# Slot attention with a switch FFN on one core: the first group's closing sums and routing placed ahead of the second group's last half, the candidate product ahead of the experts, and the end copied in halves and gated on DVE

## The reference

```
slots = layernorm(x)
k, v = rmsnorm(ctx) @ Wk.T, rmsnorm(ctx) @ Wv.T
three times:
    q = rmsnorm(slots) @ Wq.T
    attn = softmax over the 512 slots of (q . k * SCALE)
    attn = attn / (sum over the 32 context rows + eps)
    u = attn @ v
    r = sigmoid(u@Wir + h@Whr + b);  z = sigmoid(u@Wiz + h@Whz + b)
    n = tanh(u@Win + b + r * (h@Whn + b));  h = (1 - z) * n + z * h
x = x + slots
t = layernorm(x);  logits = t @ Wg        (8 experts)
gate = softmax(logits) at its argmax;  pos = tokens before this one with the same choice
keep the token if pos < 64                (capacity)
out = x + gate * ( gelu_tanh(t @ W1[e]) @ W2[e] )     for kept tokens
```

## Time and profile before

| | us |
|---|---|
| median of 3 runs | 138.66 (138.54 to 139.07) |
| profiled execution | 138.64 |
| its span | 136.9 |
| busy: PE / PE weight loads | 124.2 / 89.0 |
| busy: DVE / ACT / POOL | 93.6 / 79.4 / 33.6 |

### The profile page before, as it was taken

One profiled execution on the slowest core, in us unless ns is written; L12 is line 12 of the kernel. 1 busy time (PEld: TensorE's weight loads), 2 busy tenths in 40 slices (PEclk: granted clock), 3 DMA queues, 4 the chain that ended last, 5 costly groups with the idle time before them and its releaser, 6 DMA issues.

```text
span 136.9 us, 2770 instructions
## 1 busy us (share of the span) xinstructions
PE 124.2 (91%) x1038; PEld 89.0 (65%) x1039; DVE 93.6 (68%) x304; ACT 79.4 (58%) x154; POOL 33.6 (25%) x54
## 2 busy tenths in 40 slices
PE   6999988999899998998978997699999999999950
PEld 2573843664664754754834943599999799987830
DVE  2797656996996996996997899974782041134751
ACT  1568383945855865765636678863694265315350
POOL 7633805005005005005000060027000065550000
PEclk9999999999999999999999999999999999999998
DMA  3989991000000000000000000000101201113115
GB/s 98 277 226 333 366 382 51 0 0 7 0 0 0 0 5 0 0 2 0 5 0 0 0 0 0 0 5 0 41 5 38 77 24 30 34 31 87 34 42 153
DMA packets 9197, 8.05 MB, mean 59 GB/s; under 512 B 601, under 2 KB 7028, under 8 KB 9184
## 3 DMA queue, kind: packets, MB, share of 16 engines
q1 hardware_dynamic: 8492, 7.28, 16.6%
q0 software_dynamic: 256, 0.40, 1.2%
q10 hardware_dynamic: 436, 0.20, 0.6%
HBM read 6.43 MB, written 1.57 MB: 58 GB/s over the span
## 4 chain that ended last, share of the span: by engine, by line
PE 71%; DVE 14%; ACT 9%; issue 3%; POOL 1%; ACTq 0%; DVEq 0%
PE ps L1302 11%; PE ps L1288 11%; PE ps L1144 6%; PE ps L1117 6%; PE ps L1136 5%; PE ps L1110 5%; PE ps L980 3%; PE ps L1314 3%; PE ps L1218 3%; ACT r_b L422 3%; PE ps L1063 3%; PE ps L1181 2%; PE ps L1093 2%; ACT z_b L436 2%; PE ps L1074 2%
## 5 line engine op out<-in xcount | busy, mean ns | idle before, releaser
L1144 PE MATMUL ps<-attn,VW 32*128 32x256 f32 x144 | 12.9, 426 | 3.5 <-DVE ps L712 2.0
L1288 PE MATMUL ps<-h,W_t 128*128 128x128 f32 x128 | 15.9, 279 | 0.0
L1288 PEld LDWEIGHTS ps<-h,W_t 128*128 128x128 f32 x128 | 15.0, 192 | 0.5 <-issue 0.3
L429 ACT ACTIVATE ps<-ps,half_b 128x512 f32<-128x512 f32 x12 | 7.9, 660 | 12.7 <-PE ps L1117 12.7
L1136 PE MATMUL ps<-h,whhT 128*128 128x256 f32 x48 | 13.7, 405 | 0.0
L1117 PE MATMUL ps<-h,whhT 128*128 128x256 f32 x48 | 13.3, 398 | 0.0
L346 POOL DMA_INDIRECT y_tok<-y_rows,row_of x8 | 8.3, 1034 | 18.9 <-DMA y_rows<-y_sb 14.1
L1144 PEld LDWEIGHTS ps<-attn,VW 32*128 32x128 f32 x144 | 5.6, 182 | 10.6 <-DVE ps L712 4.4
L1110 PE MATMUL ps<-h,whhT 128*128 128x256 f32 x48 | 11.7, 384 | 0.0
L422 ACT ACTIVATE r_b<-ps,half_b 128x512 f32<-128x512 f32 x12 | 7.6, 684 | 7.1 <-PE ps L1144 7.1
L712 DVE SCALAR_TENSOR_TENSOR ps<-r_b,ps 128x512 f32<-128x512 f32 x12 | 7.8, 693 | 5.1 <-ACT r_b L422 5.1
(11 more groups left out here) (168 smaller groups left out, 255.2 us busy)
## 6 DMA issues: line engine op xcount, KB each, us to landing
W_t<-in_L_ffn_W_dram SPq DMA_DIRECT2D x1, 2048.0 KB, 9.6
x_tok<-in_x_dram SPq DMA_DIRECT2D x4, 256.0 KB, 3.9
out_dram<-h SPq DMA_DIRECT2D x4, 256.0 KB, 2.3
y_rows<-y_sb SPq DMA_DIRECT2D x4, 128.0 KB, 1.8
n_b<-in_L_xattn_gru_whh_dram SPq DMA_DIRECT2D x1, 192.0 KB, 4.1
n_b<-in_L_xattn_gru_wih_dram SPq DMA_DIRECT2D x1, 192.0 KB, 3.5
y_tok<-y_rows,row_of POOLq DMA_INDIRECT x8, 3.7
n_b<-in_ctx_dram ACTq DMA_DIRECT2D x1, 64.0 KB, 2.9
```

The lines of the kernel that those rows point to most:

```text
L1144: last = mm(to[:, hf, :], VW[g][p:p + M, gate * P:(gate + 1) * P], attn[g][p:p + M, :], start=False, stop=True, skip_group_check=True)
L1288: last = mm(hid_bank[e][:, j * BG * CAP:(j + 1) * BG * CAP], W1_t[:, ex_, j * P:(j + 1) * P], rhs, start=True, stop=True)
```

## The change

**At half 4** (t = 2, g = 0) PE no longer issues `slots_z(1, 1, 2)`, and DVE issues `final_x(0)` and `final_x(1)` each behind its `new_slots`, ahead of the denominators of the last half.

**The last half**: on PE `x2_back(0)`, `x2_back(1)` and the first group's logits stand first, then `attn_r`. The update gate's products go by a new function, `last_update`, into banks 4 and 5, one batch at a time with `positions(0)` between; batch 2's waits for the update tanh of batch 3. Fourteen filler products become three. `attn_n` stands behind `dispatch(1)`. On DVE the first group's routing stands ahead of `reset_hn`, `kept_slots` and `weigh_n`. ACT does both resets and `update(1)` ahead of `x2_norm(0)`, and `update(0)` and the two candidates behind `dispatched_out(1)`, the second candidate between `gelu(0)` and `gelu(1)`.

**The experts**: `x_T(2)` and `x_T(3)` stand behind `up(1)`, and `final_x(2)` and `(3)` read x from PSUM, without ACT's copy. `x2_back(2)`, `x2_back(3)` and the second group's logits stand behind `down(0)`.

**The end**: batches 2 and 3 are both copied on ACT, in halves of 256 columns; the transposes wait for halves and go to two banks for each batch; all eight gated additions are DVE's; batch 3 is sent in two DMAs.

```diff
     HS = [(hf, i) for hf in range(2) for i in range(BG)]
+    SLOT_HALF = [slice(0, NH), slice(NH, N)]
     SQ = 32
...
         row_bank = [bank[4], bank[5]]
-        disp_bank = [bank[2], bank[3], bank[0], bank[1]]
+        disp_bank = [bank[6], bank[7], bank[0], bank[1]]
         x_bank = [bank[6], bank[7]]
         norm_bank = [ps[:, 6, :], ps[:, 7, :], ps[:, 6, :], None]
-        late_x_bank = [bank[1], bank[0]]
+        late_x_bank = [bank[4], bank[5]]
+        last_ZV = [ps[:, 4:6, NH:N], ps[:, 4:6, 0:NH]]
         vw_bank = [bank[2], bank[3]]
-        hid_bank = [bank[2], bank[3]]
-        y_bank = [bank[6], bank[7]]
-        back_bank = [bank[0], bank[1], bank[2], bank[3]]
+        hid_bank = [bank[6], bank[7]]
+        y_bank = [bank[2], bank[3]]
+        back_bank = [[bank[2], bank[3]], [bank[0], bank[1]]]
...
             return BG * g + i
+
+        def update_bank(g, i, t):
+            return last_ZV[i] if (g, t) == (NG - 1, ITERS - 1) else ZV[i]
...
                              y_sb[:, k, :, :]).then_inc(y_put, 16)
-            for b in range(B):
-                sp.wait_ge(fin, (C, 2 * C, 3 * C, 3 * C + 1)[b])
+            for b in range(B - 1):
+                sp.wait_ge(fin, C * (b + 1))
                 sp.dma_start(out[b].rearrange("(c p) d -> p c d", p=P),
                              res[:, b, :].rearrange("p (c d) -> p c d", d=D)).then_inc(out_done, 16)
-            sp.wait_ge(out_done, 16 * B)
+            for k in range(2):
+                cs = slice(2 * k, 2 * k + 2)
+                sp.wait_ge(fin, C * (B - 1) + 2 * k + 2)
+                sp.dma_start(out[B - 1].rearrange("(c p) d -> p c d", p=P)[:, cs, :],
+                             res[:, B - 1, :].rearrange("p (c d) -> p c d", d=D)[:, cs, :]).then_inc(out_done, 16)
+            sp.wait_ge(out_done, 16 * (B + 1))
...
                 act.wait_ge(xTp, b + 1)
-                nc.scalar.activation(xT[:, b, :], (x_bank[b] if b < 2 else late_x_bank[b - 2])[:, :],
-                                     ACT.Copy).then_inc(xTc, 1)
+                nc.scalar.activation(xT[:, b, :], x_bank[b][:, :], ACT.Copy).then_inc(xTc, 1)
...
                     act.wait_ge(S[1]["scP"], 1)
-                nc.scalar.activation(halves(z_b[:, b, :]), ZV[i], ACT.Tanh, bias=half_b[:, 1:2],
+                nc.scalar.activation(halves(z_b[:, b, :]), update_bank(g, i, t), ACT.Tanh, bias=half_b[:, 1:2],
                                      scale=0.5).then_inc(s["tz"], 1)
...
             t, g = ITERS - 1, NG - 1
+            x2_out(0)
+            x2_out(1)
             reset(g, 0, t)
...
             update(g, 1, t)
-            update(g, 0, t)
-            candidate(g, 0, t)
-            candidate(g, 1, t)
-            x2_out(0)
-            x2_out(1)
-            x_out(2)
-            x_out(3)
             x2_norm(0)
...
             x_high(1)
+            dispatched_out(0)
             gate_exp(0)
             gelu_table()
-            dispatched_out(0)
             dispatched_out(1)
...
                 if s == 1:
-                    act.wait_ge(x2T, B)
+                    act.wait_ge(S[0]["h_ready"], BG * (ITERS + 1))
                 if s >= 2:
...
                 act.wait_ge(accD, b - BG + 1)
-                nc.scalar.activation(oT[:, b, :], acc_bank[b % BG][:, :], ACT.Copy).then_inc(oTs, 1)
-
-            x2_out(2)
+                for cs in SLOT_HALF:
+                    nc.scalar.activation(oT[:, b, cs], acc_bank[b % BG][:, cs], ACT.Copy).then_inc(oTs, 1)
+
+            update(g, 0, t)
+            candidate(g, 0, t)
             gelu(0)
-            x2_out(3)
+            candidate(g, 1, t)
             gelu(1)
             y_out(0)
+            x2_out(2)
+            x2_out(3)
             x2_norm(2)
...
             summed_out(2)
-            act.wait_ge(gt, 2)
-            act.wait_ge(backP, B - BG)
-            for c in range(C):
-                n = (B - 1) * C + c
-                nc.scalar.activation(oT[:, B - 1, c * P:(c + 1) * P], back_bank[B - 1][:, c * P:(c + 1) * P],
-                                     ACT.Copy, scale=gate[:, n:n + 1]).then_inc(go, 1)
+            summed_out(3)
...
                 g, i = b // BG, b % BG
-                dve.wait_ge(xTc, b + 1)
+                dve.wait_ge(xTc if b < BG else xTp, b + 1)
                 dve.wait_ge(S[g]["h_ready"], BG * ITERS + i + 1)
-                v.scalar_tensor_tensor(out=xT[:, b, :], in0=h[:, b, :], scalar=0.5, in1=xT[:, b, :],
+                v.scalar_tensor_tensor(out=xT[:, b, :], in0=h[:, b, :], scalar=0.5,
+                                       in1=xT[:, b, :] if b < BG else late_x_bank[b - BG][:, :],
                                        op0=ALU.mult, op1=ALU.add).then_inc(x2T, 1)
...
                 new_slots(g, 0, t)
+                if (g, t) == (0, ITERS - 1):
+                    final_x(0)
                 new_slots(g, 1, t)
+                if (g, t) == (0, ITERS - 1):
+                    final_x(1)
                 inv_denominators(og, ot)
...
             t, g = ITERS - 1, NG - 1
-            final_x(0)
-            final_x(1)
-            reset_hn(g, 0, t)
-            reset_hn(g, 1, t)
-            kept_slots(g, 1, t)
-            kept_slots(g, 0, t)
-            weigh_n(g, 0, t)
             x2_stats(0)
...
             x_low(1)
+            reset_hn(g, 0, t)
+            reset_hn(g, 1, t)
+            kept_slots(g, 1, t)
+            kept_slots(g, 0, t)
+            gates(0)
+            weigh_n(g, 0, t)
             weigh_n(g, 1, t)
             new_slots(g, 0, t)
+            new_slots(g, 1, t)
             final_x(2)
-            new_slots(g, 1, t)
             final_x(3)
-            gates(0)
...
             def gated_out(b):
-                dve.wait_ge(backP, b - BG + 1)
                 for c in range(C):
                     n = b * C + c
-                    v.scalar_tensor_tensor(out=res[:, b, c * D:(c + 1) * D], in0=back_bank[b][:, c * D:(c + 1) * D],
+                    dve.wait_ge(backP, 2 * ((n - BG * C) // 2) + 2)
+                    v.scalar_tensor_tensor(out=res[:, b, c * D:(c + 1) * D], in0=back_bank[b - BG][c // 2][:, c % 2 * D:(c % 2 + 1) * D],
                                            scalar=gate[:, n:n + 1], in1=x2_tok[:, n, :],
...
             gates(1)
-            dve.wait_ge(accD, BG)
-            v.tensor_copy(oT[:, B - 1, :], acc_bank[BG - 1][:, :]).then_inc(oTv, 1)
             dve.wait_ge(gt, 2)
-            gated_out(B - 2)
-            dve.wait_ge(go, C)
-            v.tensor_tensor(res[:, B - 1, :], oT[:, B - 1, :],
-                            x2_tok[:, (B - 1) * C:B * C, :].rearrange("p c d -> p (c d)"), ALU.add).then_inc(fin, 1)
+            gated_out(2)
+            gated_out(3)
...
                 if b == 2:
-                    pe.wait_ge(S[1]["n"], BG * ITERS)
+                    pe.wait_ge(S[1]["tz"], BG * ITERS)
                 to = x_bank[b] if b < 2 else late_x_bank[b - 2]
...
                     pe.wait_ge(S[1]["h_ready"], 1)
-                mm(sum_ps, fold[:, :], esum[g][:, 0:1], start=(g == 0 and t == 0), stop=True,
+                mm(sum_ps, fold[:, :], esum[g][:, 0:1], start=(g, t) in ((0, 0), (NG - 1, ITERS - 1)), stop=True,
                    skip_group_check=True).then_inc(s["fold"], 1)
...
                     last = mm(den_ps[rows, :], einv[g][rows, 0:1].broadcast_to([M, M]), ex[g][rows, :],
-                              start=False, stop=True, skip_group_check=True)
+                              start=(g, t) == (NG - 1, ITERS - 1), stop=True, skip_group_check=True)
                 last.then_inc(s["den"], 1)
...
+            def last_update(i):
+
+                g, t, b = NG - 1, ITERS - 1, batch(NG - 1, i)
+                if i == 1:
+                    pe.wait_ge(x2c, BG)
+                else:
+                    pe.wait_ge(S[g]["tz"], BG * t + 1)
+                for hf in range(2):
+                    mm(last_ZV[i][:, hf, :], whhT[:, P:2 * P], h[:, b, hf * NH:(hf + 1) * NH], start=True, stop=False,
+                       skip_group_check=True)
+                attn_gate(g, i, 1, last_ZV[i]).then_inc(S[g]["zp"], 1)
+
             def attn_n(g, t):
...
-                if b < 2:
-                    pe.wait_ge(S[1]["tz"], BG * ITERS)
                 pe.wait_ge(x2T, b + 1)
...
                 if g == 0:
-                    pe.wait_ge(S[1]["tz"], BG * ITERS)
+                    pe.wait_ge(S[1]["einv"], ITERS)
                 else:
...
-                if b < BG:
-                    pe.wait_ge(S[1]["n"], BG * ITERS)
-                else:
+                if b >= BG:
                     pe.wait_ge(x2c, B)
...
                 attn_n(g, t)
-                slots_z(og, 1, ot)
+                if (og, ot) != (NG - 1, ITERS - 1):
+                    slots_z(og, 1, ot)
                 slots_r(og, 0, ot)
...
             t, g = ITERS - 1, NG - 1
-            attn_r(g, t)
-            slots_z(g, 0, t)
-            attn_z(g, t)
-            attn_n(g, t)
             x2_back(0)
...
```

(35 more changed lines are left out.)

## The result

The changed kernel took 137.19 us in the median of 4 runs (135.46 to 139.74), the kernel before 138.60: a ratio of 0.986 (0.982 to 0.991). Two later comparisons gave 0.976 (0.972 to 0.980) and 0.986 (0.981 to 0.991). The ratios leave out the disturbed runs of either kernel; here these are part of the finding, because most of them are the changed kernel's own, by a fall of TensorE's clock.

| mean clock | runs | us |
|---|---|---|
| 0.991 to 1.000 | 6 | 135.29 to 135.77 |
| 0.986, 0.987 | 4 | 136.56 to 137.60 |
| 0.951 to 0.954 | 6 | 139.74 to 141.57 |
| 1.000 | 1 | 137.72 |

A forecast was written before the change was run, and what follows sets the result against it. The prediction took PE's work from up(0) on as the bound: up(0) 4.6 us earlier leaves 1.8, the end gives 1.0, so 138.64 - 1.8 - 1.0 = 135.8 us. Range 134.7 to 138.7.

The forecast's parts named there:

- The sum: Whole kernel: 138.64 less 1.8 at the expert stretch and 1.0 at the end gives 135.8; chance 0.58.
- the 4.6 us: First group's routing ahead of attention's last half: up(0) starts at 84.7 where it was 89.33, 4.6 earlier.
- the loss to waits: Expert stretch: second group's chain up to gelu(3) makes PE wait 0.2, 0.1 and 0.6, the last ahead of down(3).
- The 1.6 of moved work: Expert stretch: x_T (1.1) and x2_back(2) (0.55) move into it and take 1.6 of the 4.6 gained.
- the likeliest case: The sum of 135.8 holds, own range 134.8 to 136.8; chance 0.58.
- rival B: Second group's serial chain to gelu(3) slips further, three operations 0.4 late make 1.2: 137.0; chance 0.18.
- rival C: Gelu's table doesn't serve tanh, so four table loads of 1.28 are added: 138.6, no change; chance 0.12.
- The narrow gate products of one batch: Last half's update gate on PE, ahead of positions(0): four narrow products, taken as about 0.45.
- The last DMA: Kernel's end: half as large, 128 KB in 1.8 against 256 KB in 2.3; bounds 0 and 0.5, taken as 0.3.
- The end in all: Copies, transposes and gated additions save 0.68 and the last DMA 0.3, together 1.0.
- My own sign of an error: The forecast is wrong if, among other signs, PE's granted clock is under 1.00 between 74 and 100.
- rival D: Added table loads idle PE, the clock drops to 1.2 GHz for up(1) and down(0): 142.3; chance 0.12.

The follow-up runs named there:

- The experiments on the chain: Changed kernel with three of four second-group normalization operations per batch left out: 135.07 without a fall; separately, with batch 2's shift inside choose(1): mean 135.09 without a fall.
- the run of the end alone: Kernel before with only the new end (half copies on ACT, gated additions on DVE, batch 3 in two DMAs): 137.91 median of 12, ratio 0.994.
- two of the later kernels: Changed kernel without the three fillers ahead of dispatch(0), profiled at 140.50; changed kernel with batch 2's shift moved inside choose(1), its slowest run 141.46.
- five kernels with fillers put back: Changed kernel with fillers in the narrow stretch, where PE waits, there plus early shift, in both narrow stretches plus shift, and more of them: upper-clock runs 134.91 to 136.88.
- four kernels without: The changed kernel, and it without fillers ahead of dispatch(0), with a shortened second-group normalization, or with batch 2's shift earlier: best runs 135.29, 135.71, 135.07, 134.78.
- the early shift: Changed kernel with DVE's shift for batch 2 inside choose(1), behind the subtraction: 134.78 to 135.28 in four runs without a fall; others 137.14, 139.24, 141.46.
- the kernel with most fillers: Kernel with early shift and fillers in gaps and both narrow stretches, raised to six between logits(0) and logits(1), four between logits(2) and logits(3): 136.32 to 136.88.

## Why the prediction was right, and where not

*The sum.* Without a fall, the kernel takes 135.3 to 135.8; predicted 135.8. The steps, measured in the run at 135.77: up(0) at 84.49 (84.7), normalization at 95.85 (96.23), gelu(3)'s end at 102.43 (102.8), down(3)'s at 104.45 (104.7), DVE's last end at 131.42 (131.7, which is 133.49 less the 1.8). Of the 4.6 us only 1.8 would be left at down(3), said the sum; 2.1 were. ACT's work from the normalization to gelu(3)'s end took 6.58, where I took 6.56; it began 0.4 earlier than I had it, and PE waited 0.32 ahead of down(3) and not 0.6. The experiments on the chain confirm the loss to waits. The 1.6 of moved work was not tried by itself.

*The median is not the sum's.* 137.19 lies in the range I gave, but outside the likeliest case's own 134.8 to 136.8, near rival B's 137.0. But B's slip of the second group's chain didn't come, since that chain ran 0.4 earlier than forecast, and neither did rival C, for which the range reached to 138.7. That the range holds the median is luck. For "faster" I had given 0.74; the comparisons came out 1.4, 2.4 and 1.4% below the kernel before, where the sum said 2.0%, and these ratios don't count the long falls.

*Mis-sized terms.* The narrow gate products of one batch (x4 records, two products; I called them four) take 0.70, all that those of both batches take (x8), where I took 0.45; place(0) still had room. The last DMA gave 0.1 where I took 0.3; why isn't shown, though others are in flight beside it. The end in all is 0.8 by the profiles (1.0), and 0.9 by the run of the end alone.

*Tables.* Rival C is out: one load serves gelu and the tanh behind it in every profile. Nothing in the old trace could say so. What the Trainium skill has on it ("ScalarE: Activation LUTs", "Table sets: the hidden batching unit") lists tanh with other sets and is silent on this one; "What ACT_TABLE_LOAD costs" has a switch at 2.66, load and drain, and here the load takes 1.28 and the next operation starts 0.01 behind it. The prediction's "some 4 us longer" by that figure is low, since four times 2.66 less 1.40 is 5.0; nothing else rests on it.

*The clock.* This is the step that failed: the sum holds only while the clock does, and I had no term for its loss apart from rival C's idle. I wrote that no idle of the new order was over 0.7 and took that as cover, and I tied a fall to rival C's idle. The clock fell without it, in 10 of 17 runs, and in the profiled one PE had no gap in the 2 us before; the last one was of 0.23, ahead of x2_back(1). My own sign of an error, a clock under 1.00 between 74 and 100, is what came. A short fall costs 1.6 (137.1 against 135.5), the runs with a long one 4.2 to 6.0, and both profiles at 0.951 (140.50 and 141.46 us, of two of the later kernels) have a short fall behind the long one. The prediction's range doesn't hold these runs. That removed fillers "had held the clock" I offered as a remark inside rival D, whose price is worked out with C's idle. What differs is this: the change put eight transposes and the logits' eight narrow products (x16) ahead of the gates, thinned the work behind them, and took 11 fillers out. In the old order the same narrow products stood behind the gates and ahead of eight more transposes and the fillers, and no run of it had a fall. In 29 runs of five kernels with fillers put back there was no long fall, in 38 runs of four kernels without there were 14. Short falls stayed (8 of the 29). Which of the two, the place of the logits or the thinner work behind them, brings the fall isn't separated: all five have two fillers behind x2_back(0), and four of them have more behind the gates too. The small waits of 0.23 and 0.25 that stand ahead of the first and the second fall are a rival that no run tries by itself. Against it speak the old order, where PE waits 0.24 ahead of the same transposes and logits, and the kernel with most fillers, which kept the 0.25: neither had a fall. So that the clock's fall makes the difference between the runs is shown, and that fillers rid the kernel of the long ones; what brings a fall on stays open.

## What to carry to other kernels

When work is reordered, add to the sum of waits a look at what PE does in each stretch of a few microseconds: a row of PE that is busy all the time, with narrow products, is no proof that the clock will hold. Take the distribution, not one profile: the changed kernel's mean over 17 runs was 137.9, its profile without a fall 135.8. And compare kernels by all their runs: with the early shift, fillers made the best run 0.6 slower and the mean of six runs 0.9 faster than that of seven without. And when an early start is won, follow the next serial chain over the engines to the product that needs it, before counting the gain.

## What the runs showed of the hardware that was not expected

- TensorE's clock fell to 1.2 GHz with PE's matmul row busy for 2.00 of 2.00 us ahead of it, from 71.5 to 73.5, behind products of 8 columns with 128 x 128 weights.
- A fall was 3.4 us long in three profiles of runs at 0.987 (73.9 to 77.3 in two, 94.3 to 97.7 in one) and 10.2 in two others (74.4 to 84.7 and 75.0 to 85.2, each with a second fall of 3.4 later), the first stretch with nearly the same order of work in all that fell there.
- An execution can lose 2.0 us near its start with a granted clock of 1.00: products up to 9.6 us took 0.63 in place of 0.38, or 1.06 in place of 0.60.
- One activation table held the tanh-approximated gelu and tanh: one load of 1.28 us served both.
- The two 32-row products of one batch's gate take as long as the four of both batches: 0.70 (x4) and 0.71 (x8).
